# Indirect transfers that read the index tables themselves, in a graph network on one core

## The chip, the core and the metric

The kernel runs on one core of a Trainium2 chip. The core has five engines that work side by side, each with its own instruction queue: TensorE (matrix products, PE in the profile), VectorE (DVE), ScalarE (ACT), GpSimd (POOL) and SyncE (SP, which here only issues transfers). Data lies in SBUF (128 partitions), PSUM and HBM; transfers between HBM and SBUF run on 16 DMA engines. The metric is the time of one execution on the device, in microseconds.

## The reference

Four graph networks run one after the other over the same graph of 100,000 nodes (32 features each) and 25,000 edges that are sorted by destination. Each is applied to `relu(layernorm(x))` and added to `x`. What matters here is the pattern that all of them share: read the row of a source node for every edge, sum the messages by destination, compute on the nodes.

```python
def reference(x, src, dst, edge_attr_32, edge_attr_4, edge_type_8, ...):
    h = jnp.maximum(_layernorm(x, axis=-1), 0.0)
    ...
def sage_conv(x, edge_index, W_l, b_l, W_r, num_segments):   # network 0, two layers
    agg = jax.ops.segment_sum(x[src], dst, num_segments=num_segments)
    return agg @ W_l.T + b_l + x @ W_r.T
def _gcn_conv(x, src, dst, norm, W, b, n_nodes):             # network 1, three layers
    h = x @ W
    msg = h[src] * norm[:, None]
    return jax.ops.segment_sum(msg, dst, num_segments=n_nodes) + b
...
    # network 2: an edge network makes a 32x32 matrix for each edge, then 6 GRU steps
    # network 3: two layers, weights chosen by edge type
```

## The kernel before

Only nodes with an edge need messages. Every edge has a slot, and the kernel works on two spaces of slots, S (by source) and D (by destination). The slots stand in EB = 13 blocks of 2048 (T = 4 feature groups of W = 512 columns), and a block has TILES = 16 tiles of 128 slots. Nodes without messages are computed separately, in NP = 13 groups of 8192 rows: EARLY = 2 of them right after the setup (pass `N_early`), the other 11 near the end (pass `N`).

The program is written out by hand: a block of instructions for each engine, with waits on semaphores, unrolled. The passes follow each other on every engine: the setup with a scatter of run ends (`T_setup`, then `N_early` and `ENDS`), P0 (features of both ends of each edge, and the edge matrices, which are stored to HBM), P1 and P2, P3, T3 and P4, P5, the GRU passes P6 to P10, P11 and R11, P12, `N`, and P13 (results scattered to the output). Between passes the sums of the runs are written to an HBM tensor `table` (SP does this, and raises `s_table` when all have landed), and the next pass reads it with indirect transfers.

All indirect transfers are issued by GpSimd, one for each tile: 16 for a block, each with 128 row numbers, one for a partition. The row numbers lie in SBUF from the beginning, in four tables of 128 x 208 int32: `idx["src"]`, `idx["dst"]`, `idx["row"]`, `idx["run_end"]`. Before the change a block's 16 columns are first copied on GpSimd into a small buffer (`slot[par]`, `slot_d[par]`), GpSimd waits for the copy (`s_slot`), and the transfers take their row numbers from there. `fetch` (L683 to L696) does this for all gathers; `gather` (L752) calls it for P1 to P3 and P5 to P12; `body` at L743 calls it twice for a block of P0, and P4 (L782) and P13 (L803) have their own copies at L784 and L804. A gather of a block may start when TensorE has read the block two before it (`spent(..., "head", ..., 2)`, whose buffer it overwrites). In P5 and the GRU passes each single gather of block 2 and later also waits for a product of VectorE (`pace`).

Two pieces in the setup go beyond that. The scatter (body at L703) copies the row numbers (L705) and the pairs to be written (L706, from `ends` to `pair_slot`), issues 16 transfers into the HBM tensor `last_of`, and waits until they have landed, before the next block. The gather of pairs (L716 to L738) reads `last_of` at the sources into `pair_slot[par]`, and `keep_pairs` copies a landed block into the table `src_ends` (L723), two blocks behind. ScalarE and VectorE wait for all of it (`s_pairs`) before pass `ENDS`.

Of the kernel before, what the change touches and what calls it, by code (L numbers as in the profile page):

```python
# [22 lines left out]
P = 128  # L23
W = 512
Q = W // P
T = 4
D = 32
# [192 lines left out]
def gnn_kernel(nc, ins, out):  # L220
# [23 lines left out]
    with ExitStack() as ctx:  # L244
# [20 lines left out]
        s_const, s_idx, s_bd, s_start, s_slot, s_settled = one("s_const"), one("s_idx"), one("s_blockdiag"), one("s_start"), one("s_slot"), one("s_settled")  # L265
# [42 lines left out]
        slot = [sb(f"idx_slot{k}", [P, TILES], I32) for k in (0, 1)]  # L308
        pair_slot = [sb(f"pair_slot{k}", [P, TILES, 2]) for k in (0, 1)]
# [3 lines left out]
        slot_d = [sb(f"idx_slot_d{k}", [P, TILES], I32) for k in (0, 1)]  # L313
# [369 lines left out]
        def _(pool):  # L683
            slots = [0]
# [18 lines left out]
            def body(i, par, j):  # L703
                ready(pool, "tab_rm", par, q.n("tab_rm", par, j))
                nc.gpsimd.tensor_copy(slot[par][:], idx["run_end"][:, bass.ds(i * TILES, TILES)]).then_inc(s_slot, 1)  # L705
                nc.gpsimd.tensor_copy(pair_slot[par][:], ends[:, bass.ds(i * TILES, TILES), :]).then_inc(s_slot, 1)  # L706
                pool.wait_ge(s_slot, i * 2 + 2)
                settle(pool)
                for k in range(TILES):
                    pool.indirect_dma_start(last_of, bass.IndirectOffsetOnAxis(ap=slot[par][:, k:k + 1], axis=0),  # L710
                                            pair_slot[par][:, k, :], None, bounds_check=NODES - 1, oob_is_err=False
# [5 lines left out]
            slots[0] = 2 * EB  # L717
# [1462 lines left out]
```

## Time and profile before

| | us |
|---|---|
| three runs | 10668.07, 10676.45, 10708.61 |
| median | 10676.45 |
| profiled execution, whole | 10688.02 |
| profiled execution, its span | 10686.0 |

| engine | busy us | share of the span |
|---|---|---|
| TensorE | 7247.1 | 68% |
| VectorE | 4837.7 | 45% |
| GpSimd | 3509.7 | 33% |
| ScalarE | 2641.3 | 25% |

The profiled execution has 2 us around its span and lies within the three runs. TensorE's granted clock was 0.815 of full speed over the span. The passes stand at these times of the span, read from GpSimd's copies and transfers: scatter 102 to 412 us, gather of pairs 413 to 704, first gathers of P0 704 to 790 and the rest of them 944 to 1650, P1 1783 to 2110, P2 2168 to 2495, P3 2545 to 2828, P4 3021 to 3506, P5 from 3565, the GRU passes from 4216, P11 6963 to 7320, P12 7643 to 8046, `N` until 10369, P13 until the end.

An instruction's row gives its start, its duration, engine, line, what it writes and reads, and in brackets how long its engine sat idle before it and what ended that. "DMA_INDIRECT" on POOL is the time in which GpSimd makes the descriptors of one transfer; the data move later.

### The profile page before, as it was taken

What the parts mean: (1) busy time and instruction counts of PE and PEld (TensorE: products, weight loads), DVE (VectorE), ACT (ScalarE), POOL (GpSimd) and SP (SyncE); (2) the same over time, 40 slices, a digit from 0 to 9 for tenths busy, and PEclk for the clock granted to TensorE, in tenths of its full rate; (3) what the DMA queues carried; (4) which work ended last, traced back from release to release, by engine and by line L of the source; (5) the groups of instructions that cost most, each with busy time, mean ns of one, the idle gap of its engine ahead of it and who ended that gap; (6) DMA issues with size and microseconds to landing.
All of it is one profiled execution on the core that took longest, in us unless ns stands there. A gap on an engine that the chain in (4) does not pass through costs nothing.

```text
span 10686.0 us, 70568 instructions
## 1 busy us (share of the span) xinstructions
PE 7247.1 (68%) x21217; PEld 3096.3 (29%) x21226; DVE 4837.7 (45%) x7229; ACT 2641.3 (25%) x4201; POOL 3509.7 (33%) x3839
## 2 busy tenths in 40 slices
PE   3537776632388787878787787856548888788860
PEld 1213332221133222222222222224334444444430
DVE  4304222122344455757666676735545434434530
ACT  1313222110122111111111111122114455445540
POOL 4762443555434332434343424352240000000016
PEclk9757777855699898989888888878778888888875
DMA  2002444576743676767777776731120000000000
GB/s 62 9 5 78 148 152 132 52 72 63 77 94 68 144 224 187 227 203 219 215 206 228 196 237 184 228 45 20 17 8 5 16 8 8 16 8 8 8 17 19
DMA packets 529983, 1045.89 MB, mean 98 GB/s; under 512 B 100463, under 2 KB 273987, under 8 KB 529220
## 3 DMA queue, kind: packets, MB, share of 16 engines
q1 hardware_dynamic: 412292, 966.36, 25.5%
q0 software_dynamic: 117312, 75.04, 14.4%
q8 instruction: 170, 2.79, 0.1%
q14 instruction: 209, 1.71, 0.1%
HBM read 825.85 MB, written 215.77 MB: 97 GB/s over the span
## 4 chain that ended last, share of the span: by engine, by line
PE 55%; issue 13%; DVE 13%; another core or an unknown queue 9%; POOL 4%; DMA 4%; ACT 2%; SPq 0%; DVEq 0%; POOLq 0%; ACTq 0%
PE ps L911 9%; PE ps L825 5%; PE ps L1082 3%; PE ps L887 3%; PE ps L1023 3%; PE ps L1024 3%; POOL gathered L695 2%; PE ps L1027 2%; PE ps L830 2%; PE ps L836 2%; PE ps L1012 2%; PE ps L1009 2%; PE ps L899 2%; PE ps L1015 2%
## 5 line engine op out<-in xcount | busy, mean ns | idle before, releaser
L695 POOL DMA_INDIRECT gathered<-table,idx_slot x2288 | 2219.8, 970 | 1982.3 <-DVE ring L1737 1039.6
L911 PE MATMUL ps<-ring,mats 128*32 128x512 f32 x4160 | 1118.2, 664 | 437.8 <-DVE scan L1644 259.2
L1737 DVE TENSOR_TENSOR ring<-ring,ps 128x1024 f32<-128x1024 f32 x1040 | 1241.1, 1216 | 297.1 <-DMA ring<-net 200.7
L825 PE MATMUL ps<-mats,w 128*128 128x128 f32 x1820 | 380.1, 363 | 832.5 <-DVE w L2084 256.8
L825 PE MATMUL ps<-mats,gathered 128*128 128x128 f32 x1196 | 227.5, 327 | 818.3 <-DMA gathered<-table,idx_slot 543.9
L804 POOL COPY idx_slot<-idx_run_end 128x16 int32<-128x16 int32 x13 | 2.6, 196 | 2341.0 <-SPq L677 2324.5
L911 PEld LDWEIGHTS ps<-ring,mats 128*32 128x32 f32 x4160 | 210.9, 116 | 1239.2 <-issue 668.8
L825 PEld LDWEIGHTS ps<-mats,w 128*128 128x128 f32 x1820 | 280.4, 185 | 933.3 <-issue 363.3
L1082 PE MATMUL ps<-w,en 128*128 128x512 f32 x832 | 463.8, 710 | 123.5 <-issue 51.1
L688 POOL COPY idx_slot<-idx_row 128x16 int32<-128x16 int32 x143 | 29.1, 203 | 1472.6 <-SPq L493 1177.8
L1679 DVE SCALAR_TENSOR_TENSOR w<-ps,bias,w 128x512 f32<-128x512 f32 x156 | 117.1, 751 | 753.7 <-PE ps L1253 436.2
L825 PEld LDWEIGHTS ps<-mats,gathered 128*128 128x128 f32 x1196 | 162.6, 165 | 999.9 <-DMA gathered<-table,idx_slot 538.8
L887 PE MATMUL ps<-ring,mats 128*32 128x512 f32 x832 | 374.9, 630 | 60.1 <-DVE scan L1644 44.5
L1606 DVE TENSOR_SCALAR var<-ps 128x16 f32<-128x16 f32 x247 | 43.0, 175 | 812.0 <-PE ps L836 475.1
L1897 DVE TENSOR_SCALAR ring<-ps,en2b 128x512 f32<-128x512 f32 x208 | 155.6, 751 | 522.4 <-PE ps L1082 241.4
L1023 PE MATMUL ps<-blocks,wts 128*128 128x512 f32 x312 | 220.8, 798 | 190.5 <-DVE blocks L1816 180.9
L1800 DVE TENSOR_TENSOR x_block<-x_block,w 128x512 f32<-128x512 f32 x26 | 18.0, 692 | 669.1 <-ACT w L1382 622.8
L830 PE MATMUL ps<-x_block,mats 128*128 128x512 f32 x338 | 213.6, 759 | 157.4 <-DVE x_block L2061 63.0
L1082 PEld LDWEIGHTS ps<-w,en 128*128 128x128 f32 x832 | 176.6, 224 | 417.1 <-issue 280.2
L1806 DVE SCALAR_TENSOR_TENSOR w<-ps,bias,w 128x512 f32<-128x512 f32 x156 | 117.1, 751 | 383.7 <-PE ps L1027 364.6
L790 POOL DMA_INDIRECT gathered<-table,idx_slot x208 | 201.0, 966 | 256.9 <-PE ps L825 194.8
L1720 DVE TENSOR_TENSOR ring<-ring,ps 128x1024 f32<-128x1024 f32 x208 | 244.1, 1214 | 80.9 <-PE ps L877 74.6
(298 smaller groups left out, 13949.0 us busy)
## 6 DMA issues: line engine op xcount, KB each, us to landing
ring<-net SPq DMA_DIRECT2D x1248, 512.0 KB
net<-ring SPq DMA_DIRECT2D x208, 512.0 KB
table<-w SPq DMA_DIRECT2D x195, 256.0 KB, 2.9
gathered<-table,idx_slot POOLq DMA_INDIRECT x2496
x_sp<-x_block SPq DMA_DIRECT2D x117, 256.0 KB
x_block<-x_sp SPq DMA_DIRECT2D x117, 256.0 KB
d_block<-d_sp SPq DMA_DIRECT2D x104, 256.0 KB
d_block<-d_sp POOLq DMA_DIRECT2D x52, 256.0 KB, 3.1
```

The source lines that it names most:

```text
L695: pool.indirect_dma_start(dests(k), None, rows, bass.IndirectOffsetOnAxis(ap=dst[:, k:k + 1], axis=0)).then_inc(done, 16)
L825: last = nc.tensor.transpose(dst[:, k * P:k * P + P], src[:, k * P:k * P + P], mat["ident"])
L830: mm(b.centred, mat["center"], b.x, start=True, stop=True).then_inc(sig["ln_c"][b.u], 1)
L836: last = mm(b.small[:, k * T:k * T + T], b.w[0][:, k * P:k * P + P], member_mean, start=True, stop=True)
L887: last = mm(message[t * D:t * D + D, :], adders[2 * m + c], ring[slot][:, c * W:c * W + W], start=(m == 0 and c == 0), stop=(m == PAIRS // ...
L899: mm(copied4[t], mats[t * D:t * D + D, MATS.index("copies"), :], h[S_][t * D:t * D + D, col(i)], start=True, stop=True).then_inc(sig["hrm" ...
L911: last = mm(message[t * D:t * D + D, :], adders[2 * m + c], ring[slot][:, c * W:c * W + W], start=(m == 0 and c == 0), stop=(m == PAIRS // ...
L1023: mm(b.a, wt["hr"], b.new, start=True, stop=True).then_inc(sig["gr"][b.u], 1)
L1024: mm(b.b, wt["hz"], b.new, start=True, stop=True).then_inc(sig["gz"][b.u], 1)
L1082: mm((pB, pC)[k % 2][b], en2[:, c * P:c * P + P], w[0][t % 2][:], start=True, stop=True).then_inc(sig["wep"][b], 1)
L1720: v.tensor_tensor(pair, pair, state, ALU.mult).then_inc(sig["pr"][S_], 1)
L1737: v.tensor_tensor(pair, pair, state, ALU.mult).then_inc(sig["pr"][S_], 1)
```

## The change

Nothing is computed differently. Each indirect transfer now takes its row numbers straight from its column of the whole table (`index[:, i * TILES + k : ...]`). The copies at L688, L705, L784 and L804, the waits on `s_slot`, the buffers `slot` and `slot_d` and the semaphore go. The scatter reads its pairs in `ends` itself, so the copy at L706 goes; its wait for `tab_rm` and its wait for its 16 transfers to land stay. The gather of pairs writes `src_ends` directly, so `keep_pairs` and its copy at L723 go; a block still waits until the block two before it has landed, and `s_pairs` counts to 13, not 15.

```diff
@@ setup @@
-        slot = [sb(f"idx_slot{k}", [P, TILES], I32) for k in (0, 1)]
-        pair_slot = [sb(f"pair_slot{k}", [P, TILES, 2]) for k in (0, 1)]
-        slot_d = [sb(f"idx_slot_d{k}", [P, TILES], I32) for k in (0, 1)]
@@ fetch @@
-            def fetch(i, index, dst, rows, dests, done, base, per, sub, pace=None):
-
-                nc.gpsimd.tensor_copy(dst[:], index[:, bass.ds(i * TILES, TILES)]).then_inc(s_slot, 1)
-                pool.wait_ge(s_slot, i * per + (base + sub + 1))
-                settle(pool)
+            def fetch(i, index, rows, dests, done, pace=None):
+
                 for k in range(TILES):
                     if pace and i > 1:
                         pool.wait_ge(sig["pr"][S_], pace.n("pr", S_, i - 2, k) + 1 + CREDIT)
                         settle(pool)
-                    pool.indirect_dma_start(dests(k), None, rows, bass.IndirectOffsetOnAxis(ap=dst[:, k:k + 1], axis=0)
+                    pool.indirect_dma_start(dests(k), None, rows,
+                                            bass.IndirectOffsetOnAxis(ap=index[:, i * TILES + k:i * TILES + k + 1], axis=0)
                                             ).then_inc(done, 16)
@@ scatter of the setup @@
                 ready(pool, "tab_rm", par, q.n("tab_rm", par, j))
-                nc.gpsimd.tensor_copy(slot[par][:], idx["run_end"][:, bass.ds(i * TILES, TILES)]).then_inc(s_slot, 1)
-                nc.gpsimd.tensor_copy(pair_slot[par][:], ends[:, bass.ds(i * TILES, TILES), :]).then_inc(s_slot, 1)
-                pool.wait_ge(s_slot, i * 2 + 2)
-                settle(pool)
...
                 pool.wait_ge(s_sc[par], (j + 1) * (16 * TILES))
                 settle(pool)
@@ gather of pairs @@
-            def keep_pairs(i, par, j):
-                pool.wait_ge(s_tg[par], (j + 1) * (16 * TILES))
-                settle(pool)
-                nc.gpsimd.tensor_copy(src_ends[:, bass.ds(i * TILES, TILES), :], pair_slot[par][:]).then_inc(s_pairs, 1)
...
+            def body(i, par, j):
+                if j:
+                    pool.wait_ge(s_tg[par], j * (16 * TILES))
+                    settle(pool)
+                    pool.sem_inc(s_pairs, 1)
+                fetch(i, idx["src"], last_of, lambda k: src_ends[:, i * TILES + k, :], s_tg[par])
+            sweep(pool, EB, body)
@@ P4 and P13: the same, without their copies @@
-                nc.gpsimd.tensor_copy(slot[par][:], idx["row"][:, bass.ds(i * TILES, TILES)]).then_inc(s_slot, 1)
-                nc.gpsimd.tensor_copy(slot[par][:], idx["run_end"][:, bass.ds(i * TILES, TILES)]).then_inc(s_slot, 1)
@@ ScalarE and VectorE @@
-            act.wait_ge(s_pairs, EB + 2)
+            act.wait_ge(s_pairs, EB)
```

What each engine's queue holds is the same in both programs for TensorE, VectorE, ScalarE and SyncE, apart from line numbers. On GpSimd, the gather of pairs in the setup stood like this (`pair_slot0` and `idx_slot0` are the buffers of even blocks, `s_tg0` counts their landed transfers):

```order
L688 COPY idx_slot1<-idx_src 128x16 [waits s_pairs]
L695 DMA pair_slot1<-last_of,idx_slot1 128x2 [waits s_slot]
L695 DMA pair_slot1<-last_of,idx_slot1 128x2 x15
L723 COPY src_ends<-pair_slot0 128x32 [waits s_tg0]
L688 COPY idx_slot0<-idx_src 128x16 [waits s_pairs]
L695 DMA pair_slot0<-last_of,idx_slot0 128x2 [waits s_slot]
L695 DMA pair_slot0<-last_of,idx_slot0 128x2 x15
```

and now stands like this, from the first block on:

```order
L687 DMA src_ends<-last_of,idx_src 128x2 [waits s_sc0]
L687 DMA src_ends<-last_of,idx_src 128x2 x31
L687 DMA src_ends<-last_of,idx_src 128x2 [waits s_tg0]
L687 DMA src_ends<-last_of,idx_src 128x2 x15
L687 DMA src_ends<-last_of,idx_src 128x2 [waits s_tg1]
```

Both copies between two blocks are gone, and the wait for the block two before stands at a block's first transfer. The scatter ahead of it, on the same engine, stood like this:

```order
L705 COPY idx_slot<-idx_run_end 128x16 [waits s_sc0,q71]
L706 COPY pair_slot<-ends 128x32
L710 DMA last_of<-pair_slot,idx_slot 106496x2 [waits s_slot]
L710 DMA last_of<-pair_slot,idx_slot 106496x2 x15
L705 COPY idx_slot<-idx_run_end 128x16 [waits s_sc1,q70]
```

and now:

```order
L699 DMA last_of<-ends,idx_run_end 106496x2 [waits s_sc0,q71]
L699 DMA last_of<-ends,idx_run_end 106496x2 x15
L699 DMA last_of<-ends,idx_run_end 106496x2 [waits s_sc1,q70]
L699 DMA last_of<-ends,idx_run_end 106496x2 x15
L699 DMA last_of<-ends,idx_run_end 106496x2 [waits s_sc0,q71]
```

The wait for the landed transfers (`s_sc0`, `s_sc1`) moved from the copy to the first transfer.

## Rows read from the trace of the kernel before

**Rows 1.** Page, part 1: busy time, share of the span, instructions of each engine.

```profile
PE 7247.1 (68%) x21217; PEld 3096.3 (29%) x21226; DVE 4837.7 (45%) x7229; ACT 2641.3 (25%) x4201; POOL 3509.7 (33%) x3839
```

**Rows 2.** GpSimd's groups by form: busy us, mean ns; idle before.

```profile
L695 POOL DMA_INDIRECT gathered<-table,idx_slot x2288 | 2219.8, 970 | 1982.3 <-DVE ring L1737 1039.6 <-issue 621.9 <-DVE ring L1720 281.6
L710 POOL DMA_INDIRECT last_of<-pair_slot,idx_slot x208 | 210.5, 1012 | 72.6 <-issue 64.8 <-POOL pair_slot L706 7.8
...
L695 POOL DMA_INDIRECT pair_slot<-last_of,idx_slot x208 | 198.5, 954 | 78.9 <-issue 66.4 <-POOL idx_slot L688 7.3 <-remote 5.3
```

**Rows 3.** GpSimd in order of time, pairs, one block to the next: start us, us.

```profile
456.52 0.94 POOL L695 DMA_INDIRECT pair_slot<-last_of,idx_slot  x1 [0.31 <-issue]
457.47 0.22 POOL L723 COPY src_ends<-pair_slot 128x32 f32<-128x32 f32 x1
457.85 0.20 POOL L688 COPY idx_slot<-idx_src 128x16 int32<-128x16 int32 x1 [0.17 <-issue]
458.83 0.97 POOL L695 DMA_INDIRECT pair_slot<-last_of,idx_slot  x1 [0.79 <-issue]
```

**Rows 4.** GpSimd in order of time, scatter: a block's first copy and first transfer.

```profile
150.76 0.20 POOL L705 COPY idx_slot<-idx_run_end 128x16 int32<-128x16 int32 x1 [1.40 <-DMA last_of<-pair_slot,idx_slot]
...
151.96 0.99 POOL L710 DMA_INDIRECT last_of<-pair_slot,idx_slot  x1 [0.85 <-issue]
```

**Rows 5.** GpSimd, TensorE, P4: gathers behind a met wait, behind a stalled one.

```profile
3027.93 0.94 POOL L790 DMA_INDIRECT gathered<-table,idx_slot  x1 [0.30 <-issue]
...
3040.14 0.60 PE L825 MATMUL ps<-mats,gathered 128*128 128x128 f32 x4
...
3041.52 0.94 POOL L790 DMA_INDIRECT gathered<-table,idx_slot  x1 [3.91 <-PE ps L825]
```

**Rows 6.** GpSimd and TensorE in order of time, P1, around a stall.

```profile
1995.20 0.94 POOL L695 DMA_INDIRECT gathered<-table,idx_slot  x1 [0.30 <-issue]
...
2007.87 1.09 PE L825 MATMUL ps<-mats,gathered 128*128 128x128 f32 x4 [2.19 <-DVE scan L1644]
...
2009.13 0.20 POOL L688 COPY idx_slot<-idx_row 128x16 int32<-128x16 int32 x1 [12.99 <-PE ps L825]
```

**Rows 7.** TensorE, ScalarE in order of time: `N_early`, then `N` (last row).

```profile
605.41 1.88 PE L1009 MATMUL ps<-h,wts 128*128 128x512 f32 x4
...
622.95 0.69 ACT L1375 ACTIVATE w<-ps,bias 128x512 f32<-128x512 f32 x1 [21.71 <-issue]
...
8145.43 0.69 ACT L1375 ACTIVATE w<-ps,bias 128x512 f32<-128x512 f32 x1 [0.17 <-PE ps L1009]
```

**Rows 8.** Chain that ended last, shares by line: 413 to 790 us, then P3.

```profile
by line: another core or an unknown queue 62.7%; issue 26.7%; ACT w L1375 1.5%; PE ps L830 1.2%; PE ps L825 1.0%; ACT h L1375 0.9%; ACT h L1379 0.9%; PE ps L1012 0.9%; PE ps L836 0.7%; PE ps L996 0.5%; PE ps L997 0.5%; ACT h L1382 0.4%; DVE
...
by line: POOL gathered L695 67.7%; issue 28.6%; DMA gathered<-table,idx_slot 2.5%; POOL idx_slot L688 0.9%; another core or an unknown queue 0.8%; DMA table<-w 0.8%; POOLq L375 0.1%; SPq L375 0.0%; SPq L493 0.0%
```

**Rows 9.** GpSimd's waits, P1, then P2: us in total, times, longest.

```profile
POOL idx_slot L688 <- PE ps L825: 37.8, 3, 13.0
POOL idx_slot L688 <- remote: 12.0, 4, 5.9
...
POOL idx_slot L688 <- PE ps L825: 42.2, 4, 14.5
...
POOL idx_slot L688 <- remote: 2.9, 2, 2.7
```

**Rows 10.** Chain, pieces in order of time: P0, P1, P6.

```profile
1248.42 9.07 another core or an unknown queue
...
1982.95 17.54 another core or an unknown queue
...
4255.42 16.88 another core or an unknown queue
```

**Rows 11.** ScalarE and GpSimd in order of time, P13, start of a block.

```profile
10422.16 0.60 ACT L1592 ACTIVATE d_block<-ps 128x512 f32<-128x512 f32 x1 [22.36 <-POOLq L815]
...
10423.63 0.98 POOL L809 DMA_INDIRECT out_dram<-d_block,idx_slot  x1 [1.25 <-ACT d_block L1592]
```

More of the change, by code:

```diff
@@ L264, in gnn_kernel @@
         dma.update(sems(["ld_n", "st_out"], CHAINS))
-        s_const, s_idx, s_bd, s_start, s_slot, s_settled = one("s_const"), one("s_idx"), one("s_blockdiag"), one("s_start"), one("s_slot"), one("s_settled")
+        s_const, s_idx, s_bd, s_start, s_settled = one("s_const"), one("s_idx"), one("s_blockdiag"), one("s_start"), one("s_settled")
         s_pairs = one("s_pairs")
@@ L704, in body @@
                 ready(pool, "tab_rm", par, q.n("tab_rm", par, j))
-                nc.gpsimd.tensor_copy(slot[par][:], idx["run_end"][:, bass.ds(i * TILES, TILES)]).then_inc(s_slot, 1)
-                nc.gpsimd.tensor_copy(pair_slot[par][:], ends[:, bass.ds(i * TILES, TILES), :]).then_inc(s_slot, 1)
-                pool.wait_ge(s_slot, i * 2 + 2)
-                settle(pool)
                 for k in range(TILES):
-                    pool.indirect_dma_start(last_of, bass.IndirectOffsetOnAxis(ap=slot[par][:, k:k + 1], axis=0),
-                                            pair_slot[par][:, k, :], None, bounds_check=NODES - 1, oob_is_err=False
+                    pool.indirect_dma_start(last_of, bass.IndirectOffsetOnAxis(ap=idx["run_end"][:, i * TILES + k:i * TILES + k + 1], axis=0),
+                                            ends[:, i * TILES + k, :], None, bounds_check=NODES - 1, oob_is_err=False
                                             ).then_inc(s_sc[par], 16)
@@ L746, in body @@
                     spent(pool, "head", u, q3.n("head", u, i), 2)
-                    fetch(i, idx[name], (slot if u == S_ else slot_d)[par], x_rows,
-                          lambda k: G[par][u][:, k * D:k * D + D], dma["ld_g0"][2 * u + par], slots[0], 2, u)
+                    fetch(i, idx[name], x_rows, lambda k: G[par][u][:, k * D:k * D + D], dma["ld_g0"][2 * u + par])
             sweep(pool, EB, body)
-            slots[0] += 2 * EB
             def gather(name, tables_before):
@@ L761, in body @@
                         spent(pool, "head", S_, q.n("head", S_, i), 2)
-                    fetch(i, idx["row"], slot[par], table.rearrange("r (t f) -> (r t) f", t=T),
-                          lambda k: G[par][S_][:, k * D:k * D + D], dma["ld_gs"][par], slots[0], 1, 0,
+                    fetch(i, idx["row"], table.rearrange("r (t f) -> (r t) f", t=T),
+                          lambda k: G[par][S_][:, k * D:k * D + D], dma["ld_gs"][par],
                           q if name == "P5" or name in GRU_PASSES else None)
                 sweep(pool, EB, body)
-                slots[0] += EB
             for k in (1, 2, 3):
@@ L791, in body @@
                             G[t % 2][S_][:, k * P:k * P + P], None, table4.rearrange("r t f -> (r t) f"),
-                            bass.IndirectOffsetOnAxis(ap=slot[par][:, k * T + t:k * T + t + 1], axis=0)
+                            bass.IndirectOffsetOnAxis(ap=idx["row"][:, i * TILES + k * T + t:i * TILES + k * T + t + 1], axis=0)
                         ).then_inc(dma["ld_g4"][t % 2], 16)
             sweep(pool, EB, body)
-            slots[0] += EB
             for k in range(5, 13):
@@ L809, in body @@
                     pool.indirect_dma_start(out.rearrange("r (t f) -> (r t) f", t=T),
-                                            bass.IndirectOffsetOnAxis(ap=slot[par][:, k:k + 1], axis=0),
+                                            bass.IndirectOffsetOnAxis(ap=idx["run_end"][:, i * TILES + k:i * TILES + k + 1], axis=0),
                                             db[D_][:, k * D:k * D + D], None, bounds_check=NODES - 1, oob_is_err=False
@@ L1869, in _ @@
             q = p_["ENDS"]
-            dve.wait_ge(s_pairs, EB + 2)
+            dve.wait_ge(s_pairs, EB)
             settle(dve)
```

18 lines of the change are left out of this document (2 added, 16 removed).

## The prediction

> **What bounds the kernel now.** I read the busy times first [rows 1]: no engine is full, so the question is what each pass waits for. GpSimd is busy for 33%, and nearly all of that is making descriptors [rows 2]. Then the waits and the chain of waits, pass by pass. In P3 the chain is GpSimd itself: 67.7% gathers and 28.6% the pauses between them [rows 8]. In the GRU passes the table's gathers wait for VectorE's ring products [rows 2], so GpSimd is early there, except at a pass's start. In pass N no transfer of GpSimd runs at all.
>
> The rest is less plain. While GpSimd sends gather after gather, whoever waits for TensorE waits long. In the second group of N_early TensorE has four L1009 products done at 607.3, and ScalarE's L1375, which needs them, starts at 622.95; in pass N the same step costs 0.17 us [rows 7]. From 413 to 790 us, 89% of the chain is unnamed or "issue" [rows 8]. Long pieces of the same kind stand in P0, P1 and P6, and one in P1 ends shortly after a stream of gathers does: the last gather ends at 1996.14, and the chain moves on at 2000.49 [rows 6, 10]. I take it that TensorE's signals come late while indirect transfers stream, and that the end of a stream sets them free. So GpSimd's stream is on the path in passes where it seems to have slack.
>
> The ends of TensorE's rows are no proof that a product was done. The Trainium skill (Perfetto Trace Analysis, "Tensor Engine Instruction") says that such an end is worked out from the instruction's size, and that the signal goes out only when PSUM has acknowledged the writes. By it the 15 us may be real work that the rows hide and not a late signal; the sum is the same either way, since only the time at which the waiter starts is used.
>
> **What one copy costs.** There are three cases.
> Inside a stream, gathers are 0.30 us apart. With both copies of the pair stage, one gather ends at 457.46 and the next starts at 458.83: 1.37 us, so 1.07 go if the wait that stays, met long ago, costs nothing [rows 3]. In P4 the first gather of a quarter has such a wait and no copy: the one at 3027.93 follows after 0.30 [rows 5]. With the index copy alone it is 0.20 + 0.78 = 0.98 us, and 0.68 go.
> Behind a wait on TensorE that stalls: the copy starts 0.17 us after the head's end (2008.96 to 2009.13) and its first gather 0.98 later [rows 6, 3]; a gather without a copy starts 0.78 after the head's end [rows 5]. So 1.15 becomes 0.78: 0.37 us go.
> Behind the drain of the scatter: the first transfer starts 1.20 us after the first copy, some 1.36 after the landing [rows 4]; in P13 a scatter transfer starts 0.87 us after what it waits for [rows 11]. So 0.50 us go.
>
> **The sum, stage by stage.**
> Scatter: 13 x 0.50 = 6.5 us of GpSimd. TensorE's first group of nodes runs beside it, and the time removed is a pause in which TensorE is free. I count 0, with bounds 0 and 6.5.
> Pairs, and the first two blocks of P0: 0.68 + 11 x 1.07 + 0.5 at the drain + 3 x 0.68 = 15.0 us. The path is N_early's second group, which gets on slowly until 790; a stream that ends 15 us sooner gives 15 us at full speed and takes away 15 us at the slow one. By the 11% of the chain that is named work [rows 8], and some more for safety, I put the slow speed at a fifth: 12 us. Bounds 0 and 15.0.
> P0: eleven more blocks, each with one copy inside the stream and one behind a stall: 11 x (0.68 + 0.37) = 11.6 us if the stream is the path, 0 if TensorE is. A piece of 9.07 us near the end of a stream shows that the first happens [rows 10]; how much of a block is like it one row doesn't tell. I take half of the inner copies: 3.7 us.
> P1: the start, three stalls on TensorE and four short ones marked remote are 8 blocks at 0.37, and 5 are left at 0.68: 6.4 us; P2: 7 at 0.37 and 6 at 0.68: 6.7 us [rows 9]. In a stalled block the removed pause is one in which TensorE moves at full speed, so I take three quarters of the 7.5 of inner copies and 30% of the 5.6 of the others: 7 us. Bounds 0 and 13.1.
> P3: GpSimd is the path [rows 8]: 0.37 + 12 x 0.68 = 8.5 us, taken whole.
> P4: its start, 0.4 us. Later copies stand behind waits for a head a quarter ahead, and VectorE and TensorE have work in between.
> P5 to P10, six starts: the first two blocks stream, and TensorE is stuck for 16.88 us at their end [rows 10]: 6 x (0.37 + 0.68) = 6.3, of which I take 5.4 us. After that each gather waits for VectorE, and the copy lies inside that wait.
> P11: its start, 1.0 us. Later blocks stall behind TensorE: the copy is removed from a pause, and I count 0; bound 5.0 with the start.
> P12: a start of four blocks, 0.37 + 3 x 0.68 = 2.4, and pairs of blocks after it, each with a copy inside its stream: 5 x 0.68 x 0.6 = 2.0, a share between those of P0 and P1. Together 4.4 us, bound 2.4 + 5 x (0.37 + 0.68) = 7.6.
> P13: 0. The copy runs beside ScalarE's L1592, which both programs wait for: it ends at 10422.76, after the copy. If that cover were gone, a block would gain 0.5 us, 6.5 in all.
> The sum is 0 + 12 + 3.7 + 7 + 8.5 + 0.4 + 5.4 + 1.0 + 4.4 = 42.4, so 42 us. The profiled execution took 10688.02, 12 more than the median; it would come to 10646, and the median of 10676.45 to **10634**.
>
> **Rivals.** *Every microsecond of stream is time.* The upper bounds add up to 6.5 + 15.0 + 11.6 + 13.1 + 8.5 + 0.4 + 6.3 + 5.0 + 7.6 = 74 us: 10602. For it speaks how sharply the chain moves on when a stream ends [rows 6, 10]; against it, that TensorE does get on inside a stream.
> *A toll for each gather.* If each gather holds TensorE up by a fixed amount, however dense they come, pauses are full-speed time for TensorE, and removing them wins nothing where TensorE is the path. P3's 8.5, P4's 0.4 and the first block of seven other starts remain, 2.6 us: 11 to 12 us, so 10664. For it: a pause is always on TensorE's side. Against it: pauses of 1.4 us seem too short for TensorE to notice.
> *The pauses feed TensorE* (slower). If signals held back get out mainly in the pauses between blocks, the pair stage loses its eleven pauses of 1.37 us. The second group advances there by a fifth of 350 us, some 70; if all of it came from the pauses, 70 us of work would be left over, less 15 for the shorter stage: 55 slower there, and with P3 and the starts 20 faster elsewhere, 10676 + 35 = 10711. It decides the sign once more than a fifth of those 70 us comes from the pauses (15 of 70). Against it: the pauses come every 21 us or so, and the chain's pieces that I looked at do not end with one; a single release, at 622.95 [rows 7], is thin ground.
> *Longer transfers.* If a transfer took longer with row numbers in rows of 832 bytes than in rows of 64, 0.68 us for a block would be eaten up at 0.68 / 16 = 43 ns for a transfer. The widest gap between transfers of these forms is 1012 - 954 = 58 ns [rows 2]; on about 1500 transfers whose stream is time that is 87 us, against 42: 10676 + 45 = 10721. Each transfer reads one number from a partition before and after, so I see no reason for it. The Trainium skill (GPSIMD Engine Reference, "Performance pitfalls for Q7 kernels") speaks for this rival: an access in steps of over 8 bytes costs half as much again for each element. No row here shows that reading apart.
> That the change doesn't do what it says is excluded: the copies are gone from GpSimd's queue.
>
> **Chances.** Forecast (30 to 55 us gained) 0.50; all of the stream 0.25; toll 0.16; pauses feed 0.04; longer transfers 0.05. The range must leave out no more than 0.2: from 10602, the full gain, to 10664, the toll; what is slower stays outside. A measurement can tell about 0.5% from no change, 53 us. Over 53 us faster: nearly all of the 0.25 and 0.08 of the forecast, 0.33. Over 53 us slower cannot come of these cases at their price, but I leave 0.04 for them being larger than priced. Within: 0.63.
>
> **What would show it.** Pauses between blocks in the pair stage and in P3 of 0.30 us; P3's gathers over some 8.5 us sooner, the pair stage 12.5; the first head of P0 some 12 us earlier; starts of the GRU passes about 1 us shorter; P13 unchanged. DMA_INDIRECT of the table at some 970 ns would refute longer transfers. N_early ending later, although its stream ends sooner, would be the pauses. If P0, P1 and P12 each shrink by the whole of their copies, I was too low; if only P3 and the starts do, too high.

## The result: 1.7% slower in the first comparison

| | before, us | changed, us |
|---|---|---|
| runs | 10668.07, 10676.45, 10684.64, 10708.61 | 10814.15, 10860.89, 10862.73, 10934.54 |
| median | 10680.55 | 10861.81 |
| profiled execution, whole / span | 10688.02 / 10686.0 | 10860.89 / 10858.8 |

The ratio is 1.0172, with a 95% interval of 1.0111 to 1.0232. 10634 was forecast, and 10602 to 10664 was the range. Further on, the same kernel is 1.2% slower when measured again, perhaps on another chip, and 0.5% faster on a chip where the kernel before itself takes 6% less. So the sign changed with the chip, or with something else that changed together with it. First the profile of the changed kernel, from the chip of this comparison.

Page, part 1, of the changed kernel; beside [rows 1] GpSimd has lost its copies (3592 instructions, 3839 before), and nothing else has less or more to do.

```profile
PE 7238.9 (67%) x21217; PEld 3096.1 (29%) x21226; DVE 4835.6 (45%) x7229; ACT 2644.3 (24%) x4201; POOL 3439.7 (32%) x3592
```

GpSimd's group of table gathers (as [rows 2]). The transfers did not get longer: 964 ns with the row numbers in the tables, 970 before.

```profile
L687 POOL DMA_INDIRECT gathered<-table,idx_row x2288 | 2205.3, 964 | 3518.1 <-SPq L490 1197.8
```

GpSimd in order of time, pair stage, one block to the next (as [rows 3]). The boundary between two blocks lies ahead of the second or third row; either gap is 0.30 or 0.31 us and no copy stands in it, so the 1.37 us pause is gone, as announced.

```profile
436.56 0.94 POOL L687 DMA_INDIRECT src_ends<-last_of,idx_src  x1 [0.30 <-issue]
437.81 0.94 POOL L687 DMA_INDIRECT src_ends<-last_of,idx_src  x1 [0.31 <-issue]
439.06 0.94 POOL L687 DMA_INDIRECT src_ends<-last_of,idx_src  x1 [0.30 <-issue]
```

ScalarE in order of time, the first node group of `N_early`, in the same stage. L1358 and L1360 each follow a product of TensorE.

```profile
545.74 0.69 ACT L1358 ACTIVATE w<-ps,bias 128x512 f32<-128x512 f32 x1 [4.79 <-issue]
551.34 0.69 ACT L1360 ACTIVATE w<-ps,bias 128x512 f32<-128x512 f32 x1 [4.91 <-remote]
556.25 0.69 ACT L1358 ACTIVATE w<-ps,bias 128x512 f32<-128x512 f32 x1 [4.23 <-remote]
561.84 0.69 ACT L1360 ACTIVATE w<-ps,bias 128x512 f32<-128x512 f32 x1 [4.90 <-remote]
```

One product arrives each 5.6 us (4.9 once); on another chip, below, they come 0.86 us apart. A GRU step has twelve of them and takes 67 us (from 545.74 to 612.94, the next step's first row). Each product is two matmul rows, which take 2.07 us together at the lower level of TensorE's clock (1.2 GHz; the row at 449.87) and 1.12 at the higher (2.4 GHz; 472.19), so the clock does not make the 5.6 us. In the kernel before, this group's six steps had ended at 390 us, before the pair stage; here the sixth ends at 724, long after. The chain of waits between 413 and 790 us (as [rows 8], where unnamed and "issue" were 89%), with its longest pieces. "Another core or an unknown queue", like "remote" in a row, is not to be taken literally in a program on one core: it stands for a wait whose signal comes too long after any row that could have sent it, and in the rows above it is the signal of a product of TensorE.

```profile
by line: another core or an unknown queue 81.0%; issue 6.7%; PE ps L995 2.3%; PE ps L793 2.0%; DVE w L1782 1.7%; DVE w L1779 1.6%; PE ps L991 1.5%; DVE h L1782 1.5%; DVE h L1779 1.5%; PE ps L992 1.4%; PE ps L804 1.2%; PE ps L798 0.9%; DMA g
...
547.74 41.38 another core or an unknown queue
614.94 41.37 another core or an unknown queue
```

The pair stage itself was shorter by more than forecast (first to last gather 287 us before, 267 after). But P0's first gather of x, which overwrites buffers that `N_early` uses, now waits 80.75 us for TensorE:

```profile
745.17 0.94 POOL L687 DMA_INDIRECT gathered<-in_x_dram,idx_src  x1 [80.75 <-PE ps L793]
```

Where the time came from, by the start of the first and the end of the last gather of each stage: the third block of P0, whose gathers wait for the setup to be done, starts at 1053 us (945 before): 108. From there to P0's last gather 741 us (701): 40. To P1's start 5 more. From P1 to P12's first gather 3. P12's gathers take 413 us (400) and the rest is 4 more. Together 173 us, the difference of the two spans.

### The profile page after: what moved, and what is told of

It reads as the page before. It is cut to its first block, busy times and chain, and to the rows that moved or that the text cites. A ratio compares the mean times of both kernels' runs of the same rounds, so it can differ in the third digit from the quotient of the medians.

```text
span 10858.8 us, 70098 instructions
## 1 busy us (share of the span) xinstructions
PE 7238.9 (67%) x21217; PEld 3096.1 (29%) x21226; DVE 4835.6 (45%) x7229; ACT 2644.3 (24%) x4201; POOL 3439.7 (32%) x3592
## 4 chain that ended last, share of the span: by engine, by line
PE 55%; DVE 13%; issue 11%; another core or an unknown queue 10%; POOL 4%; DMA 4%; ACT 2%; SPq 0%; DVEq 0%; POOLq 0%; ACTq 0%
PE ps L879 9%; PE ps L793 5%; PE ps L1050 3%; POOL gathered L687 3%; PE ps L855 3%; PE ps L991 3%; PE ps L992 2%; PE ps L798 2%; PE ps L804 2%; PE ps L995 2%; PE ps L977 2%; PE ps L980 2%; PE ps L983 2%; PE ps L867 2%
## 5 line engine op out<-in xcount | busy, mean ns | idle before, releaser
L687 POOL DMA_INDIRECT gathered<-table,idx_row x2288 | 2205.3, 964 | 3518.1 <-SPq L490 1197.8
L777 POOL DMA_INDIRECT out_dram<-d_block,idx_run_end x208 | 202.6, 974 | 2433.2 <-ACT d_block L1560 2369.6
L687 POOL DMA_INDIRECT gathered<-in_x_dram,idx_src x208 | 198.1, 952 | 669.6 <-PE ps L793 607.5
L762 POOL DMA_INDIRECT gathered<-table,idx_row x208 | 200.3, 963 | 308.6 <-PE ps L793 245.5
L1311 ACT ACTIVATE w<-w,bias 128x512 f32<-128x512 f32 x156 | 112.5, 721 | 673.1 <-DVE w L1653 615.8
```

## Two kinds of chip

The experiments (told below; their short names stand here already) ran on six chips, each with the kernel before beside it: e1 to e4 on one chip, c1, c2 and e5 on another, and f1 to f4, g1 to g3, h1 and h2, i1 and i2 on one each. On four of the six the kernel before took 10067 to 10071 us (all kernels 10026 to 10099), and TensorE's signals were on time: from the semaphore events of the traces, the median signal came 0.01 us after the end of the row that sends it, in every stage. On two (c1, c2, e5; h1, h2) and on the chip of the first comparison the kernel before takes 10643 to 10681, and in the pair stage TensorE's signals come late, while in pass `N`, which has no indirect transfers, they come after 0.01 too. That pass takes the same time on both kinds: from P12's last gather to P13's first it is 2331 us in the kernel before of the first comparison, 2330 in g2, and 2328 to 2337 in every profile of the table below. I call the two kinds prompt chips and late chips. The chip of the first comparison isn't named in its results and may be one of the two. Each chip was met for one stretch of time, so whether it is the chip or something else that lasted for that stretch is open.

How late the signals are can be told only roughly. The traces of late chips lack a part of the semaphore events: of 60 rows of VectorE in the pair stage of the kernel before that raise a semaphore, 11 have an event within 0.1 us of their end, and yet a weight load of TensorE in the changed kernel, which waits for such a row without an event, starts 0.05 us behind its end (542.24 to 542.29). The median for TensorE comes out between 6 and 13 us, by how rows without an event are counted. The starts of ScalarE's rows, which follow the signals within 0.03 us, don't have this fault.

ScalarE on a prompt chip, changed kernel (g1), pair stage, same lines as above: 0.86 us apart, beside the same stream of gathers.

```profile
478.69 0.70 ACT L1358 ACTIVATE h<-ps,bias 128x512 f32<-128x512 f32 x1
479.55 0.69 ACT L1360 ACTIVATE h<-ps,bias 128x512 f32<-128x512 f32 x1
480.40 0.69 ACT L1358 ACTIVATE h<-ps,bias 128x512 f32<-128x512 f32 x1 [0.17 <-PE ps L991]
481.26 0.69 ACT L1360 ACTIVATE h<-ps,bias 128x512 f32<-128x512 f32 x1 [0.17 <-PE ps L992]
```

And the chain there, 413 to 790 us: GpSimd's gathers themselves and the gaps between them are the path, as the forecast had it for P3 alone.

```profile
by line: POOL src_ends L687 51.6%; issue 20.2%; PE ps L1050 10.6%; POOL gathered L687 8.2%; PE ps L1041 2.6%; PE ps L793 1.5%; PE ps L798 1.3%; PE ps L804 1.0%; DMA src_ends<-last_of,idx_src 0.8%; DVE scan L1612 0.7%; DMA gathered<-in_x_dra
```

The profiled runs of the late chips and four of the prompt ones in one table. "Restart" is the start of P0's third block, "P0" the time from there to its last gather, "P12" from its first gather to its last.

| run | kernel | restart | P0 | P12 | span |
|---|---|---|---|---|---|
| first, late | before | 945 | 701 | 400 | 10686 |
| first, late | changed | 1053 | 741 | 413 | 10859 |
| c1, late | before | 943 | 676 | 382 | 10634 |
| c2, late | changed | 977 | 732 | 407 | 10763 |
| e5, late | copies kept up to P0 | 919 | 680 | 407 | 10664 |
| h1, late | copies kept, tables read | 944 | 685 | 381 | 10648 |
| h2, late | changed, pair stage drained | 817 | 737 | 409 | 10622 |
| g2, prompt | copies kept, tables read | 789 | 480 | 278 | 10062 |
| g1, prompt | changed | 756 | 482 | 277 | 10027 |
| g3, prompt | changed, pair stage drained | 788 | 483 | 280 | 10067 |
| i1, prompt | as g3, and P0 drained | 797 | 515 | 277 | 10073 |

A restart on a late chip is not a sharp number: e5 has the setup and the pair stage of c1, on the same chip, and restarts 24 us sooner. In the profiles of prompt chips with the setup of before (e1, e4, f1, f3, f4, g2) the restarts lie between 782 and 794.

## The experiments

**Theories.** *Pauses*: on late chips TensorE's signals get out in GpSimd's pauses, far beyond the pauses' own length. *Tables*: reading the row numbers from tables of 832 bytes a partition does harm. *Forecast*: the stream is the path and pauses are worth their length.

**e1: all copies and waits kept, transfers read the tables.** The copies become dead work.

```diff
-  pool.indirect_dma_start(dests(k), None, rows, bass.IndirectOffsetOnAxis(ap=dst[:, k:k + 1], axis=0)
+  pool.indirect_dma_start(dests(k), None, rows, bass.IndirectOffsetOnAxis(ap=index[:, i * TILES + k:i * TILES + k + 1], axis=0)
```

The scatter, P4 and P13 alike; the scatter also takes its pairs from `ends`, as in the changed kernel.

> The kernel before with all its copies and waits, so with every pause of GpSimd between blocks, but the indirect transfers read their row numbers (and the scatter its data) from the whole tables, as in the changed kernel; the copies are dead. If what slows the changed kernel is the loss of the pauses, this one takes the time of before, 10680 us within 30, and P0's first gather of x starts near 704. If it is the reading or the place of the row numbers, it takes the time of the changed kernel, 10860, and N_early's GRU steps fall 67 us apart.

**e2: the scatter alone changed; e3: the pair gathers alone; e4: P0's gathers alone.** Each is the kernel before with that piece as the change has it.

> The kernel before with the setup's scatter alone changed (no copies, transfers read the tables); pairs and all passes keep their copies. Pauses theory: in the scatter 13 pauses get 0.5 to 1.2 us shorter and TensorE's first node group falls back, so that its six GRU steps, which ended at 390 us just before the pair stage began, fall partly into that stage at some 60 us each. I expect 50 to 100 us of the 108 by which P0's restart was late: 10740 to 10780. If the scatter's pauses do nothing, 10674 to 10681.

> The kernel before with the pair gathers alone changed (in place, no copies). Pauses theory: N_early's second group, which lies beside this stage, loses the eleven pauses of 1.37 us; the first group's six GRU steps still end before the stage. Expected 10720 to 10790, with P0's restart 40 to 100 us later than 945. Forecast's own theory: P0's restart 12 us sooner, 10668.

> The kernel before with P0's gathers of x alone changed (no copies). Pauses theory: a block of P0 takes 70 us in place of 66, as in the changed kernel, 44 us in all: 10725, and the first two blocks save some 3 us. Forecast's theory: 4 us faster, 10677. If the late start of P0 (at 1052 in place of 945) and not the pauses made its blocks longer, its blocks stay at 66 us.

Measured, all on one prompt chip: before 10068.84; e1 10064.79 (ratio 0.9999, 0.9990 to 1.0009), e2 10062.16 (0.9992, 0.9982 to 1.0001), e3 10047.48 (0.9985, 0.9975 to 0.9994), e4 10066.31 (0.9998, 0.9989 to 1.0008). The expectations were made for a chip like the first; on this one only e3's interval leaves 1 out: the medians differ by 21 us (the ratio says 15), of which 10 to 16 lie before P0's restart (772 in place of 782 in e4 and 788 in e1). e1 tells nothing between the theories, but it says that reading the tables costs nothing here. e2, e3 and e4 were never run on a late chip, so no run there has the scatter, the pair gathers or P0 alone without their copies.

**c1, c2, e5: the kernel before, the changed one, and the passes P1 to P13 alone changed.**

> The kernel before itself, for its profile beside the next two. In e1 to e4 no signal of TensorE came late while gathers streamed (0.01 us after the end of the row, against 8.67 in the pair stage of the first profile) and the time was 10069 and not 10681. If that belongs to the chip on which a call runs, this profile is either of the one kind (some 10681 us, GRU steps of N_early 15 us apart before the pairs and the second group stuck until 790) or of the other (some 10069, P0's blocks 48 us); nothing between.

> The changed kernel itself. Where signals come late: 10862 or so again, slower than before by 1.7%. Where they do not: every microsecond taken from GpSimd's stream is time wherever GpSimd is the path, and nothing else changes: e3 gave 21, e2 7, e4 3, and P1, P2, P3 and six starts should add the forecast's terms of 7 + 8.5 + 5.4 and some of the upper bounds, so 10069 - 50 = 10019, between 10000 and 10030. If the changed kernel is slower here too, the late signals were not the cause.

> The kernel before with P1 to P13 alone changed; setup, pairs and P0 keep their copies. Where signals come late: P1, P3 shorter and P2, P12 longer as in the changed kernel, and the offset after P0 gone: 10681 + 24 - 1 = about 10700. Where they don't: 13 copies of 0.68 us in each of P1, P2 and P3 and the starts of the others: 20 to 30 us faster than before. By the forecast's terms of these passes: 7 + 8.5 + 0.4 + 5.4 + 1.0 + 4.4 = 27 us faster.

Measured, on a late chip: before 10642.92; changed 10763.02 (1.0115, 1.0080 to 1.0151); e5 10680.51 (1.0039, 1.0023 to 1.0055). So the slowdown came again, and a third of it, 38 us, comes from the passes. The table shows where: P12 takes 407 us without its copies, twice (c2, e5), and 382 with them (c1). P1 took 9 us more in e5, but 1 less in c2. For c1 I had said that nothing lies between the two kinds; its 10636 lies 45 below 10681, and it is the late kind by its signals.

**f1 to f4: e1 and e4 again, a drain in the pair stage, longer pauses in P0.** The edit of f2, in the changed kernel, makes each block wait for the landing of its own gathers:

```diff
                 fetch(i, idx["src"], last_of, lambda k: src_ends[:, i * TILES + k, :], s_tg[par])
+                pool.wait_ge(s_tg[par], (j + 1) * (16 * TILES))
+                settle(pool)
```

The edit of f4, in the kernel before, behind each copy of P0:

```diff
+                    for n in range(3):
+                        nc.gpsimd.tensor_copy(rest[:], index[:, bass.ds(i * TILES, TILES)]).then_inc(s_rest, 1)
+                        pool.wait_ge(s_rest, (i * 2 + sub) * 3 + n + 1)
```

> The kernel of e1 again (all copies and waits kept, transfers read the tables), for a chip on which TensorE's signals come late; on the other kind it told nothing of the cause. Late signals and the pauses as the cause: the time of before, within 0.3% (some 10640), the x gathers' span in P0 some 920 us. Reading the tables as the cause: 10760, x gathers over 1036. Where signals are on time: within 0.1% of before again.

> The changed kernel, but in the pair stage each block waits until its own 16 gathers have landed; no copy. So twelve pauses of 2 to 3 us stand where the kernel before had 1.37 and the changed one 0.30. If pauses of any kind let TensorE's signals out: P0's blocks restart at 943 or sooner (changed kernel 977 on the last chip, 1053 on the first), and the time falls by 30 to 100 us against the changed kernel, to 10660 to 10730. If the copies themselves and not the pause had helped, it stays at 10763 plus the 20 to 30 us of pauses. Where signals are on time: 20 to 30 us slower than the changed kernel, near 10040.

> The kernel of e4 again (P0's 26 copies gone, all else as before) for a chip with late signals. There the span of the x gathers was 920 us in the kernel before and 1036 in the changed one, of which 34 came from the late restart. Pauses in P0's own streams as the cause: 50 us slower than before (10690), a block 4 us longer. If P0's blocks are long only because of what the setup left: no change.

> The kernel before with three more copies behind each of P0's 26, each waited for, into a buffer that nobody reads: pauses of 3.0 us in place of 0.98 in the middle of a block, and as much at its start. With f3 and before this makes pauses of 0.3, 0.98 and 3.0 us. Pauses as the cause, still short of what TensorE needs: faster than before by 10 to 40 us, the block of P0 1 to 3 us shorter. Pauses saturated at 1 us, stream the path: 26 x 2.04 = 53 us slower. Where signals are on time, the stream is the path in P0: 40 to 53 us slower.

Measured, on a prompt chip again: before 10071.26; f1 10068.78 (1.0000), f2 10064.13 (0.9991, 0.9981 to 1.0001), f3 10066.49 (0.9998), f4 10075.88 (1.0004, 0.9995 to 1.0014). For the theories f1 and f3 say nothing new. f4 was a miss: I expected 40 to 53 us, and pauses of some 53 us by plan cost 5. On a prompt chip GpSimd's stream is not the path in P0.

**g1 to g3: the changed kernel, e1's kernel and f2's kernel.**

> The changed kernel itself, for the kind of chip that this call meets. Where TensorE's signals come late (first profiles, c1, c2, e5): 1.0% to 1.8% slower than before. Where they are on time (e1 to e4, f1 to f4): faster, by the sum of its parts: pairs 20 us (e3), scatter 5 (e2), P0 3 (e4) and some 20 for P1 to P3 and the starts, 48 in all, 10020.

> All copies and waits kept, transfers read the tables. Late signals: the pauses as the cause give the time of before within 0.3%; the reading of the tables as the cause gives the time of g1. On time: before within 0.1%, as twice already.

> The changed kernel with a drain behind each block of the pair stage: pauses of 2 to 3 us, no copy. Late signals: if any pause lets them out, the restart of P0 comes back from about 1000 to 943 or sooner and the time falls 30 to 100 us below g1; if only copies do, 20 to 30 us above g1. On time: 20 to 45 us above g1 (f2 gave 10064).

Measured, on a third prompt chip: before 10070.61; changed 10026.32 (0.9953, 0.9936 to 0.9969), g2 10065.65 (0.9996, 0.9986 to 1.0005), g3 10063.47 (0.9993, 0.9983 to 1.0002). On a prompt chip the change makes the kernel 44 us faster; the sum had said 42. g2 to g1 is the change without the reading of tables, and it has the whole gain.

**h1, h2: the same two kernels, on a late chip this time.**

> All copies and waits kept, transfers read the tables; a further try for a chip whose TensorE signals come late (it was met with signals on time in e1, f1 and g2, where it took the time of before). Late: pauses as the cause give the time of before within 0.3%, the x gathers' span some 920 us; reading the tables as the cause gives 1% to 1.8% more, over 1030 us.

> The changed kernel with a drain behind each block of the pair stage. Late: if any pause lets TensorE's signals out, P0 restarts near 943 or sooner, and the time is 30 to 100 us below the 1.0115 of before that the changed kernel took in c2; if only copies do, above it. On time: 10064 as in f2 and g3.

Measured: before 10649.67; h1 10643.45 (0.9988, 0.9972 to 1.0005); h2 10602.25 (0.9966, 0.9950 to 0.9983). With the copies kept and the tables read, the time is that of before: *tables* falls on late chips too. And a pause without any copy brings back more than the copies did, so it is not the copy itself that helps: P0 restarts at 817 us, against 943 with copies and 977 (1053 in the first comparison) without pauses. P0 and P12, which have no pauses in h2, take 737 and 409 us, as in the changed kernel; in h1, which has them, 685 and 381. So P0 and P12 pay for their own lost pauses: in the profiles of late chips P0 takes 676 to 701 us with its copies and 732 to 741 without, and P12 381 to 400 and 407 to 413.

How much of TensorE's work gets done beside the pair stage, 415 to 660 us in each of five kernels (busy us of PE, PEld, DVE, ACT and POOL with their instructions, then the granted clock, the DMA engines' busy share and GB/s): first the changed kernel, without pauses, then c1 and h1 with their copies, then h2 with the drain, last g2 on a prompt chip.

```profile
415.00:660.00 245.00, 62.09 (x80) 19.35 (x80) 25.38 (x37) 27.02 (x38) 185.18 (x192) 0.56 0.05 1
415.00:660.00 245.00, 89.22 (x164) 33.25 (x162) 11.81 (x36) 24.92 (x41) 173.22 (x200) 0.57 0.04 1
415.00:660.00 245.00, 103.03 (x188) 39.92 (x188) 14.68 (x55) 28.37 (x47) 173.56 (x198) 0.60 0.04 1
415.00:660.00 245.00, 152.66 (x368) 72.86 (x368) 38.70 (x113) 67.18 (x115) 165.70 (x173) 0.71 0.06 8
415.00:660.00 245.00, 135.82 (x336) 64.88 (x336) 80.77 (x139) 87.08 (x130) 181.41 (x199) 0.76 0.05 5
```

TensorE started 80 matmul rows without pauses (119 in c2), 164 and 188 with the copies (190 in the kernel before of the first comparison, 159 in e5), and 368 with the drain, no fewer than on a prompt chip (336). Most pauses of the copies are 1.37 us, but two or three of eleven are waits of 3 to 6 us, and together they make 22 us of the 245 in c1 and in h1. The eleven of h2 are 2.2 to 3.2 us and make 27. So h2 has twice the rows of h1 at little more pause in all. Besides its evener and mostly longer pauses, h2 differs in that each block's transfers have landed before the next begins. Which of the two it takes was not separated: f4, longer pauses without a drain, met a prompt chip only.

How a pause acts can be seen in the chain of c1, 590 to 625 us. GpSimd's gathers stop there from 607.70 to 612.47, mostly in a wait that the trace puts down to "remote"; the rows of GpSimd stand behind those of the chain.

```profile
595.60 4.89 another core or an unknown queue
...
600.54 5.56 another core or an unknown queue
...
606.14 5.55 another core or an unknown queue
...
611.74 2.75 another core or an unknown queue
614.53 2.06 another core or an unknown queue
```

```profile
611.14 0.20 POOL L688 COPY idx_slot<-idx_src 128x16 int32<-128x16 int32 x1 [3.21 <-remote]
612.47 0.97 POOL L695 DMA_INDIRECT pair_slot<-last_of,idx_slot  x1 [1.13 <-POOL idx_slot L688]
```

TensorE's signals had come 5.6 us apart, and come 2.8 and 2.1 apart from the end of the pause on. By the semaphore events they then come 2.8, 3.5, 3.5, 4.2 and 4.9 apart, all multiples of 0.70 us: some 20 us after the pause, about the length of a block of 16 gathers, its effect is nearly used up. The same stands in the trace of the kernel before, over the whole pair stage: two signals of TensorE that follow each other are 1.1 us apart (median) within 4 us of a block's first gather, 2.7 in the next 4, and 4.2 to 5.6 from there on (39 pairs, of the events that the trace has). In the changed kernel they are 5.3 to 6.3 apart everywhere in a block (30 pairs). In h2, behind a drain of 2.32 us, the chain names TensorE's own work (5.31 us for eight rows); 16 us behind it signals come 2.8 us apart (2.1 us of wait and 0.7 of ScalarE's row):

```profile
496.31 0.94 POOL L687 DMA_INDIRECT src_ends<-last_of,idx_src  x1 [2.32 <-DMA src_ends<-last_of,idx_src]
```

```profile
496.04 5.31 PE ps L982 x8
...
510.16 2.10 another core or an unknown queue
...
512.97 2.09 another core or an unknown queue
```

**i1, i2: more drains.** i1 drains the pair stage and each 16 gathers of P0; i2 also each block of P1, P2 and P12.

```diff
                     fetch(i, idx[name], x_rows, lambda k: G[par][u][:, k * D:k * D + D], dma["ld_g0"][2 * u + par])
+                    pool.wait_ge(dma["ld_g0"][2 * u + par], (j + 1) * (16 * TILES))
+                    settle(pool)
```

> The changed kernel with a drain (a wait for the landing of its own gathers) behind each block of the pair stage, and in P0 behind each 16 gathers of x. Late signals: in h2, which had the pair stage's drains alone, eleven blocks of P0 took 737 us, in h1 with its 1 us copies 686. If any pause lets TensorE's signals out and a longer one more of them, P0 comes to 640 to 690 and the time to 10500 to 10560 (before 10650, h2 10602). If the drains of P0 only add their own length, 26 x 2 = 52 us: 10650. On time: 10064 and up to 30 more, P0's stream being the path there.

> The same, and a drain behind each block's 16 gathers in P1, P2 and P12, where a stall on a head often follows in any case. Late signals: P12, which took 382 us in before and 409 without its copies, comes back to 382 or less, P1 and P2 stay within 10 us: 20 to 40 us below i1. If pauses do nothing there, 10 to 30 above i1. On time: P1 and P2 up to 25 us longer each, 10 to 50 above i1.

Measured, on a prompt chip: before 10067.4; i1 10063.29 (0.9997, 0.9987 to 1.0006); i2 10099.19 (1.0036, 1.0023 to 1.0048). There P0's drains cost nothing against g3, although its gathers take 515 us in place of 483: P1's first gather starts at 1391 in both. Those of P1, P2 and P12 cost 36. What i1 gives on a late chip, where it was meant to help, was not measured.

## Why the prediction was wrong

**The cost of a copy on GpSimd was right.** The pair stage's boundaries show 0.30 us, the scatter's 2.09 in place of 2.59, the 0.50 forecast.

**The step that failed** is this one of the pair stage: "a stream that ends 15 us sooner gives 15 us at full speed and takes away 15 us at the slow one". It took the slow speed, a fifth, as a constant of the stage. But the slow speed was made by the pauses: without them TensorE's rows beside the stage fall from 190 to 80 (first comparison) and from 164 to 119 (c1, c2), and two signals stand 5.3 to 6.3 us apart throughout instead of 1.1 just behind a pause. The chance of 0.04 for *the pauses feed TensorE* rested on a look at where long pieces of the chain ended, and on the view that pauses of 1.4 us were too short to notice. A pause doesn't end a piece; it makes the pieces behind it shorter, for 20 us. The distance between signals by their distance from the last pause, given above, would have shown it in the trace of before. The rival's own condition, "more than a fifth of those 70 us", was met, but it was also too low for the whole change: with the 20 us that the rival counts as gained elsewhere, the sign turns at 35 of the 70. The working also took it that the end of a stream sets the signals free. In the changed kernel it does so only after some 28 us: the last pair gather ends at 664 us, and ScalarE's rows that wait for a product come close together from 691.35 on.

```profile
680.14 0.69 ACT L1358 ACTIVATE w<-ps,bias 128x512 f32<-128x512 f32 x1 [5.49 <-remote]
685.04 0.69 ACT L1360 ACTIVATE w<-ps,bias 128x512 f32<-128x512 f32 x1 [4.21 <-remote]
689.24 0.69 ACT L1358 ACTIVATE w<-ps,bias 128x512 f32<-128x512 f32 x1 [3.52 <-remote]
691.35 0.69 ACT L1360 ACTIVATE w<-ps,bias 128x512 f32<-128x512 f32 x1 [1.42 <-remote]
691.93 0.68 ACT L1358 ACTIVATE h<-ps,bias 128x512 f32<-128x512 f32 x1
```

**The rival's price** was wrong too, 10711 where 10862 (and 10763 in c2 against 10643) were measured. It charged the pair stage alone, with 55 us; the restart came 108 and 34 us late. P0, forecast at 3.7 us of gain, lost 40 and 56 without its copies, and P12, forecast at 4.4, lost 13 and 25. The traces show where the two restarts part: in c2 the first group's six GRU steps, 15 us each, ended at 386 us, before the pair stage, and in the first comparison they fell into it, at up to 67 us each. Two delays ahead of them add up there. ScalarE's fourth round of L1343 (L1375 in the kernel before) started at 310 us, 34 later than in the kernel before, beside the scatter; in c2 it was 13 us later than in c1. Then the layer norm behind it took from 335 to 455 us, beside the rest of the scatter and the start of the pair stage, where the kernel before took 15 us and c2 19. What made the first delay that long in one run and not in the other was not looked into, and with 24 us between the restarts of c1 and e5 the 34 of c2 alone would be a thin proof.

**Prompt chips.** 42 us of gain were forecast and 44 measured, but the terms are not those of the sum. By g1 and g2, whose spans differ by 34.5, the setup gave 33 (restart 789 to 756): 13 up to the first pair gather, where I had counted 0, 16 in the pair stage, where the forecast's own terms make 12.4, and 4 from there to the restart. P0 took 1 us more in place of 3.7 less. What follows it gave 3 net, and not 27. That the total came out at 44 is luck.

**P3** is where a gain was given back. 8.5 us were forecast, GpSimd being the path, and its boundaries did shrink to 0.30 us. But its gathers took 276 us (279 before). Behind the 145th gather, the first of the tenth block, GpSimd stands still in all twenty profiles; first the kernel before, then the changed one, then g1.

```profile
2737.52 0.97 POOL L695 DMA_INDIRECT gathered<-table,idx_slot  x1 [0.78 <-issue]
2742.43 0.95 POOL L695 DMA_INDIRECT gathered<-table,idx_slot  x1 [3.94 <-issue]
```

```profile
2887.54 0.94 POOL L687 DMA_INDIRECT gathered<-table,idx_row  x1 [0.30 <-issue]
2899.40 0.94 POOL L687 DMA_INDIRECT gathered<-table,idx_row  x1 [10.92 <-issue]
```

```profile
2278.93 0.95 POOL L687 DMA_INDIRECT gathered<-table,idx_row  x1 [0.30 <-issue]
2289.14 0.94 POOL L687 DMA_INDIRECT gathered<-table,idx_row  x1 [9.27 <-issue]
```

It is 3.94 us before and 3.2 to 6.2 in the other ten profiles with copies in P3, and 10.92 in the changed kernel and 9.3 to 10.7 in the other eight without them. What it waits for no row names ("issue"). The step was right in its mechanism and missed what is late next.

**Longer transfers** is refuted on both kinds: 964 and 971 ns with the tables (970 before), h1 and g2 at the time of before. The Trainium skill (GPSIMD Engine Reference, "Performance pitfalls for Q7 kernels") charges accesses in steps of over 8 bytes with half as much again for each element; no run here shows that in a transfer that takes one number from each partition.

**Late signals or hidden work.** The Trainium skill (Perfetto Trace Analysis, "Tensor Engine Instruction") says that a row's end is worked out, and that the signal goes out when PSUM has acknowledged the writes. On prompt chips signal and worked-out end agree within 0.02 us for nine signals of ten. On late chips they lie microseconds apart, and in the stretches shown above the signals follow each other at multiples of 0.70 us. The same products beside the same stream take 0.86 us each on a prompt chip, so 5.6 us is not what such a product needs. Whether TensorE itself works more slowly on a late chip or only its signals are held up can't be told, since the ends of its rows are not observed; "late signals" is a name for either.

**Which version.** On prompt chips the changed kernel is the fastest (0.9953). On a late one it loses 1.2% or 1.7%, and h2's kernel wins (0.9966, measured on one late chip), which on prompt chips lies at 0.9991 and 0.9993: of the kernels run on both kinds the only one that gained on one and lost on none. It is no more than a tie on prompt chips, since both intervals reach 1.

## What to carry to other kernels

A wait between indirect transfers can be of use to another engine, so when one is removed, look at how fast the other engine gets on just behind such a wait and just ahead of the next one, and not only at the wait's length. Where signals of TensorE come late beside a stream of gathers, a drain of some 2.3 us after each 16 gathers made one stage 31 us longer and let the next work start 160 us sooner (h2 against c2, two chips). And measure on more than one chip before a change of 1% is called a gain or a loss.

## What the runs showed of the hardware

On two of six chips TensorE's signals come late while GpSimd issues indirect transfers, as on the chip of the first comparison; the kernel before takes 10643 to 10681 us there and 10067 to 10071 on the other four. GpSimd's own transfers take the same time on both, 970 and 971 ns. In the stretches shown the signals then follow each other at multiples of 0.70 us, up to 5.6 us for each product; a gap in the stream shortens that, and the next 16 gathers bring it back. After the last pair gather in the changed kernel, at 664 us, the signals took some 28 us to come close together again. What in the chip does this, and why only in some, was not found.
